# A fused two-layer block: preparing the output stage inside the stage before it, and finishing its last tile block by block

## The reference, cut to what matters

```
xn = layernorm(x)
x  = x + attention(xn) + gated_ffn(xn)                       # first layer
xn = layernorm(x)                                            # second layer; what follows is the change's place
proj = xn @ in_proj_w.T                                      # gate, conv channels, dt
y    = state_space_scan(silu(conv(proj)))                    # 128 heads, 8 groups, done over 8 chunks of 128 tokens
g    = y * silu(gate)                                        # 1024 tokens x 8192
g    = g / sqrt(mean(g*g over the group) + eps) * norm_w     # 8 groups of 1024 channels
a    = g @ out_w.T                                           # 8192 -> 512
base = xn @ W.T + bias                                       # the adapter layer's plain part
lora = (xn @ lora_A.T) @ (2 * lora_weights * lora_B)         # 128 rows between (8 adapters of rank 16)
out  = x + a + base + lora
```

## Time and profile before

| what | us |
|---|---|
| median of 3 executions | 2231.82 (2231.77 to 2232.87) |
| the profiled execution: its own time | 2228.98 |
| the profiled execution: its span | 2227.0 |
| last matmuls of the scan begin | 1829.15 |
| last small sums on PE begin, the only PE work up to the next row | 1835.64 |
| first LoRA matmul of the output stage begins | 1849.14 |
| first matmul on gated rows begins | 1858.62 |
| last matmul begins | 2218.32 |

### The profile page before, as it was taken

One profiled execution on the slowest core, in us unless ns is written; L12 is line 12 of the kernel. 1 busy time (PEld: TensorE's weight loads), 2 busy tenths in 40 slices (PEclk: granted clock), 3 DMA queues, 4 the chain that ended last, 5 costly groups with the idle time before them and its releaser, 6 DMA issues. The chain is left out here.

```text
span 2227.0 us, 37068 instructions
## 1 busy us (share of the span) xinstructions
PE 2108.4 (95%) x12040; PEld 1562.7 (70%) x12040; DVE 1462.8 (66%) x1813; ACT 1353.2 (61%) x2384; POOL 861.2 (39%) x758
## 2 busy tenths in 40 slices
PE   6879999898999999999999999999999987999998
PEld 4634444476777777777777777777777756888886
DVE  4446666284568677778778587786787764555555
ACT  2145555433588878888787787877888762233332
POOL 1011111121157666657666575665667570000000
PEclk9989999999999999999999999999999998999999
DMA  3422322223445445445454454455454557444462
GB/s 132 161 75 71 82 76 61 74 95 95 119 131 161 158 148 175 145 140 184 134 165 154 145 166 154 140 168 153 150 177 148 159 181 256 141 139 139 141 217 76
DMA packets 184055, 310.81 MB, mean 140 GB/s; under 512 B 20512, under 2 KB 96800, under 8 KB 183744
## 3 DMA queue, kind: packets, MB, share of 16 engines
q1 hardware_dynamic: 183872, 308.53, 44.7%
HBM read 252.52 MB, written 55.68 MB: 138 GB/s over the span
## 5 line engine op out<-in xcount | busy, mean ns | idle before, releaser
L145 PE MATMUL ssm_pp<-xhi,ssm_lo 128*128 128x512 f32 x1192 | 479.4, 402 | 4.7 <-DVE ssm_bc L1541 3.5
L147 PE MATMUL ssm_pp<-xhi,ssm_hi 128*128 128x512 f32 x1192 | 466.2, 391 | 0.0
L146 PE MATMUL ssm_pp<-xlo,ssm_hi 128*128 128x512 f32 x1192 | 465.6, 391 | 0.0
L1443 ACT ACTIVATE ssm_sct<-ssm_cumb,ssm_gpar 128x128 f32<-128x128 f32 x1024 | 312.9, 390 | 53.5 <-DMA ssm_cumb<-dt_sums 28.5
L1541 DVE SCALAR_TENSOR_TENSOR ssm_xc<-ssm_pp,vectors,ssm_xc 128x1022 f32<-128x1022 f32 (+2 forms) x192 | 245.1, 1277 | 47.3 <-ACT ssm_xc L1402 32.3
L137 POOL TENSOR_TENSOR ssm_lo<-ssm_raw,ssm_hi 128x512 fp32r<-128x512 f32 x149 | 238.0, 1602 | 93.1 <-ACT ssm_hi L126 93.1
L145 PEld LDWEIGHTS ssm_pp<-xhi,ssm_lo 128*128 128x128 f32 x1192 | 224.0, 188 | 69.0 <-issue 20.9
L147 PEld LDWEIGHTS ssm_pp<-xhi,ssm_hi 128*128 128x128 f32 x1192 | 224.2, 188 | 48.1
L146 PEld LDWEIGHTS ssm_pp<-xlo,ssm_hi 128*128 128x128 f32 x1192 | 224.3, 188 | 42.8
L1576 DVE TENSOR_TENSOR ssm_sct<-ssm_sct,ssm_cbm 128x1024 f32<-128x1024 f32 x128 | 224.5, 1754 | 40.5 <-ACT ssm_sct L1450 27.8
L1708 POOL TENSOR_TENSOR ssm_go<-ssm_t,ssm_gt 128x512 f32<-128x512 f32 x128 | 165.1, 1290 | 201.3 <-DVE ssm_t L1612 201.3
(11 more groups left out here) (210 smaller groups left out, 4011.8 us busy)
## 6 DMA issues: line engine op xcount, KB each, us to landing
ssm_cumb<-dt_sums SPq DMA_DIRECT2D x96, 1024.0 KB, 6.1
ssm_raw<-w SPq DMA_DIRECT2D x149, 256.0 KB, 5.6
gated<-ssm_go SPq DMA_DIRECT2D x128, 256.0 KB, 4.6
out_graw<-gated SPq DMA_DIRECT2D x64, 512.0 KB, 4.2
out_raw<-w SPq DMA_DIRECT2D x65, 256.0 KB, 2.7
ssm_cumb<-dt_sums SPq DMA_DIRECT2D x32, 512.0 KB, 4.0
ffn_raw<-w SPq DMA_DIRECT2D x37, 256.0 KB, 2.8
stk_qs<-qk_parts SPq DMA_DIRECT2D x96, 64.0 KB, 2.2
```

The costliest lines, as they stand in the source:

```text
L145: pe.matmul(out, wlo, xhi, start=start, stop=False)
L146: pe.matmul(out, whi, xlo, start=False, stop=False)
L147: return pe.matmul(out, whi, xhi, start=False, stop=stop)
L1443: i = act.activation(sct[:, s % 2, h, :], cumb[:, s % 2, 0, h, :], ACT.Relu, scale=-1.0, bias=gpar[:, unit, 0, s % NTOK, h:h + 1])
```

## The change

- The lora_A tile becomes the last of the five extra tiles, and lora_B becomes a sixth weight tile of the state-space feed (load, high part on ACT, low part on POOL, in slot 2 of its ring). PE multiplies nothing with it in that stage.
- The product with lora_A is not stored to `base`. ACT (`lora_high`, in the place of the fifth `copy_pre`) and DVE (`lora_low`, behind the last `finish`) read it from PSUM, scale it by the coefficient and write the two halves into slots 0 and 1 of the same ring. The coefficient is made early in the stage by DVE.
- The output stage's semaphores live through both stages, and POOL clears 30 of them at the start of the state-space stage. The clearing block and its barrier are gone.
- SP no longer waits at the end of the state-space stage. In the output stage it waits for `rstd` and `gated` before it loads them, for `squares` in step 0 of the first group, and for `base` in the last group.
- The work on group 7's 1/sqrt moves to later steps (sum from the start to j = 2, square root to j = 3, reciprocal from j = 2 to j = 4, its store from j = 3 to j = 5).
- In the last of the 64 tiles PE goes by output block with both batches inside, and signals each block. DVE takes a block when it is signalled.

```diff
@@ emit_ssm @@
-            return not (last and ... r[0] >= G) or r[1] < NPRE
+            return not (last and ... r[0] >= G) or r[1] <= NPRE
 ...
-            base_out(NPRE - 1)
             squares_out(G - 1, 0)
             out(G - 1, NS - 1)
             squares_out(G - 1, 1)
-            for q in g_out:
-                sp.wait_ge(q, G * NS // 2 * 16)
-            sp.wait_ge(rms_out, 16)
-            sp.wait_ge(pre_out, NPRE * 16)
-            sp.wait_ge(var_out, 2 * G * B * 16)
 ...
+            def lora_high():
+                act.wait_ge(dt_dve, 6 + NTOK)
+                act.wait_ge(tile_done, G * GT + NPRE)
+                act.activation(lora_h[0], slot(NE + NPRE - 1), ACT.Copy, scale=lc[:, 0:1]).then_inc(marks.lora_hi, 1)
 ...
+            def lora_low():
+                dve.wait_ge(marks.lora_hi, 1)
+                dve.scalar_tensor_tensor(lora_h[1], slot(NE + NPRE - 1), lc[:, 0:1], lora_h[0].bitcast(F32),
+                                         ALU.mult, ALU.subtract).then_inc(marks.lora_lo, 1)
 ...
+            for s in marks.cleared:
+                pool.sem_clear(s)
             for r in range(feed.begun, rank(FIRST, is_tile) + AHEAD):
                 low((0, r))
@@ emit_out, before its block @@
-        with nc.Block() as clear:
-            @clear.gpsimd
-            def _(pool):
-                for s in mine:
-                    pool.sem_clear(s)
@@ emit_out, SP @@
-            sp.dma_start(h[:], c.pre_dram[0]).then_inc(h_in, 16)
             load_w(0, 0)
+            sp.wait_ge(m.rms_out, 16)
             sp.dma_start(rs[:, 0, :], c.rs_dram[0].partition_broadcast(P)).then_inc(rstd_in, 16)
+            for q in m.g_out:
+                sp.wait_ge(q, NB * 16)
             load_g(0, 0)
             load_w(0, 1)
             load_g(0, 1)
-            load_w(0, 2)
-            for unit in range(2):
-                sp.dma_start(halves[:, unit, :], over_partitions(c.var_dram[unit, G - 1:G])).then_inc(sq_in, 16)
+            for q in m.g_out:
+                sp.wait_ge(q, G * NB * 16)
@@ emit_out, PE @@
+                if last:
+                    for o in range(KT):
+                        for b in range(B):
+                            mm = part(*args, o, b, False, True)
+                        mm.then_inc(sums_done, 1)
+                    return
 ...
-            pe.wait_ge(h_lo_done, 1)
-            spread(0, 0, h_hi, h_lo, True, False)
+            q = NPRE % lora.slots
+            h_hi, h_lo = (half[:, 0:2, :].rearrange("p s t -> p (s t)") for half in (lora.hi, lora.lo))
+            for b in range(B):
+                for o in range(KT):
+                    part(lora.hi[:, q, :], lora.lo[:, q, :], h_hi, h_lo, o, b, True, False)
@@ emit_out, DVE @@
-            dve.wait_ge(tile_done, PRE + G * NB)
             dve.wait_ge(base_added, KT)
             for o in range(KT):
+                dve.wait_ge(sums_done, o + 1)
                 dve.scalar_tensor_tensor(x[:, o, :], ps[:, o, :], c.vec[:, V_OB + o:V_OB + o + 1], x[:, o, :],
                                          ALU.add, ALU.add).then_inc(added, 1)
```

More of the change, by code:

```diff
@@ L1060, in exists @@
         def exists(r, last):
-            return not (last and isinstance(r[0], int) and r[0] >= G) or r[1] < NPRE
+            return not (last and isinstance(r[0], int) and r[0] >= G) or r[1] <= NPRE
         def made(e, last):
@@ L1069, in pre_dst @@
         def pre_dst(i):
-            return xc[:, 0, i, :] if i < CU else gt[:, 0, 0, :]
+            return xc[:, 0, i, :]
         def conv_col(g, e):
@@ L1818, in body @@
                     if not (first and j < 2):
-                        load_w(g, PRE + j)
+                        load_w(g, j)
                     if not (last and j + 2 >= NB):
                         load_g(g, j + 2)
+                    if first and j == 0:
+                        sp.wait_ge(m.var_out, 2 * G * B * 16)
+                        for unit in range(2):
+                            sp.dma_start(halves[:, unit, :], over_partitions(c.var_dram[unit, G - 1:G])
+                                         ).then_inc(sq_in, 16)
                     if first and j < G - 1:
@@ L1926, in body @@
                     if j == 2 and isinstance(g, int) and not last:
+                        dve.wait_ge(sq_in, 32)
+                        dve.tensor_tensor(sums[:], halves[:, 0, :], halves[:, 1, :], ALU.add).then_inc(sq_sum, 1)
+                    if j == 4 and isinstance(g, int) and not last:
                         dve.wait_ge(std, 1)
```

128 lines of the change are left out of this document (66 added, 62 removed).

## The result

| what | before | after |
|---|---|---|
| median of the executions timed side by side, us | 2231.82 (2229.59 to 2236.74, 5) | 2215.96 (2215.1 to 2221.35, 5) |
| ratio | | 0.9941, 95% interval 0.9925 to 0.9956 |
| the profiled execution: own time, span | 2228.98, 2227.0 | 2215.61, 2213.9 |
| issue of the last squares to the first load of the output stage | 4.16 | 0.73 |
| ... to the first LoRA matmul | 10.64 | 0.78 |

The account below looks back on a forecast made before the run. PE was taken to bound the kernel, gapless in the output stage's long part, so gains lie at its edges: 3.8 + 3.8 - 0.2 = 7.4 us, 2231.8 to 2224.4 us. Range: 2222.5 to 2226.5; 8 in 10: 2219.0 to 2227.8.

Parts of the forecast that it names:

- The block's entry: Start of the output stage: without the 0.8 us wait and 2.5 us clearing block, the first load comes 3.3 us earlier.
- The LoRA rows: Output stage's first 24 matmuls: start at 1839.4 instead of 1849.1, take 7.6 us from half clock, end at 1847.0.
- The first gated tile: After the LoRA rows: tile 1 lands at 1849.45, PE starts gated rows at 1852.8; gain at this edge 3.8 us.
- 512 KB at 403 GB/s are 1.3 us: Load queue at the output stage's start: dropping out_h brings the second load of gated rows 1.3 us earlier.
- The rival with faster loads: Output stage's start: loads avoid the small-load slowdown, PE starts at 1849.9; edge gives 8.7, sum 12.3 us; chance 0.18.
- Group 7's 1/sqrt: First steps of the output stage: moving this work by two steps was costed at nothing.
- The second start at half clock: First gated tile: after 5.8 us of PE idleness the clock is at half again, charged 2.0 us.
- No part of the change touches what is in that stretch: Long part of the output stage, 1536 matmuls at 0.2344 us: claimed untouched by the change, so no gain or loss.
- The last tile: End of the output stage: only the fourth block's addition and store follow the last matmul; gain 3.8 us.
- The state-space stage: Stage before the output stage: POOL's added low part delays ssm_xw and may hold PE; loss 0.2 us, bounds 0 and 1.3.
- contention rule: State-space stage: GpSimd contends with two-input DVE instructions, so the new low part holds DVE; sum up to 1.3 us smaller.
- The sum: Whole kernel: 3.8 + 3.8 - 0.2 = 7.4 us, span 2219.6 us, median 2224.4 us; the forecast had chance 0.60.

Follow-up runs that it names:

- clears_back: The changed kernel with the block clearing the output stage's semaphores, and its barrier, back between the stages; ratio to the kernel before 0.9955.
- wait_back: The changed kernel with SP's waits for all its stores back at the end of the state-space stage; ratio to the kernel before 0.9954.
- lora_reload: The changed kernel, again loading 512 KB from base first and splitting it into unused tiles, LoRA matmuls waiting for that; ratio to the kernel before 0.9961.
- halves_late: The changed kernel with the two small loads of squares, and SP's wait for them, two steps later; ratio to the kernel before 0.9957.
- kept_warm: The changed kernel with 12 more LoRA matmuls ahead of the real ones, result unchanged; ratio to the kernel before 0.9948.
- tail_only: The kernel before with only the last tile changed, to go by output block with its signals and DVE waits; ratio to the kernel before 0.9975.
- low_late: The changed kernel with POOL making the low part of lora_B behind its last squares; ratio to the kernel before 0.9944.

## Why the prediction was right in direction and wrong in size

- **The block's entry, forecast 3.3 us earlier: right.** The first load moved from +4.16 to +0.73, 3.4. clears_back puts the block at 2.2 where 2.5 was forecast, wait_back the wait at 0.8 to 0.9.
- **The LoRA rows: right.** They start at the barrier, at half clock, and end near 1846.8; 1847.0 was forecast.
- **The first gated tile: right chain, wrong landing.** "512 KB at 403 GB/s are 1.3 us" is the first step that failed: taking out_h away was worth 2.77 us of landing time (lora_reload). The rows of tile 1 landed 8.7 us behind the first load where 10.1 was forecast; with out_h back they took 11.5, as before (11.4). DVE multiplied tile 1 at 1847.86 instead of 1849.45, and PE started at 1851.03 instead of 1852.8. The rival with faster loads gave 8.7 us for this edge, for a cause that halves_late refutes; that its sum of 12.3 lies near the measured 13.2 is chance, since the spacing made up the difference.
- **Group 7's 1/sqrt, "I cost it at nothing": incomplete.** Its sum had held tile 1's multiplication by 1.2 us before. The forecast has this gain without naming it: it goes from the landing straight to the 3.3 us of the chain, where before had 1.26 us in between (1854.05 to 1855.31).
- **The second start at half clock: right in kind,** 1.38 instead of 2.0, and 1.4 to 2.8 over the profiles; kept_warm shows that it goes with the idle time. With the landing, the entry gave 6.15 instead of 3.8.
- **"No part of the change touches what is in that stretch": wrong, 2.9 us.** This is the second step that failed. The instructions are the same, but SBUF addresses are not, by 32 bytes. It is the largest error of the sum, which put the term at nothing. It is a lucky one: the same edit could have moved the rows to a worse distance.
- **The last tile: right,** 3.9 against 3.8, in tail_only too.
- **The state-space stage: the path was right, the size too small,** 1.05 us by low_late against 0.2, inside the bounds of 0 and 1.3. The pair of profiles before and after shows none of it, since the first profile of before was long in this step. By the nearest rows I had taken the delay of `ssm_xw` for covered; it was 1.27 of low part and 0.86 of a slower `ssm_sqs`. The prediction gave the contention rule of the Trainium skill, GPSIMD Engine Reference, section 1, as one by which DVE would be held. The trace agrees, and both engines pay. Over the stage of the changed kernel that DVE product takes 1.21 to 1.23 us in the 33 cases with no POOL operation beside it, and 2.31 (median) in the 57 with POOL busy throughout it; POOL's decay of the state takes 1.05 to 1.07 us in the 16 cases without that product beside it and 1.97 to 2.05 in the other 48. So the spread of the earlier trace rows goes with POOL. In the rows above, at the one place that counts, it was POOL that paid (1.32 for 0.46, 2.04 for 1.06), while DVE's product took 1.34 and 1.38 us. By the rule the prediction had a loss of up to 1.3 us more than its 0.2; low_late puts the whole loss at 1.05.
- **The sum:** entry 6.15, spacing 2.9, end 3.9, and 0.1 ahead of them in these two profiles: 13.1 us of span instead of 7.4. The median fell 15.9 us, 2.8 more. No experiment explains these 2.8; they are of the size of the spread of executions, and the interval of the ratio (9.8 to 16.7 us) covers them. So of the 8.4 us by which the median missed the forecast, 5.7 are terms of the sum, 2.9 of them the spacing and 2.35 the entry, and 2.8 are not explained.

## What to carry to other kernels

When an edit adds or removes any SBUF tile, compare the spacing of matmuls in a stretch that it doesn't touch, and try to put weights and moving operands a multiple of 256 bytes apart. Price a load at the head of a queue by what the same place of the trace needs for its bytes, not by the rate of a full stream. And when work is moved ahead of a barrier, look at the idle time that it leaves behind: here a filler of 12 matmuls cost nothing that the profile shows and kept the clock. Look also at what stands ahead of the critical operation in its engine's order: a small sum that waited for small loads held it by 1.2 us.

## What the runs showed of the hardware

- The spacing of 128x512 fp32r matmuls with a weight load each was 0.2267, 0.2324 or 0.2333, 0.2343 and 0.2333 us at 0, 128, 160 and 192 bytes (modulo 256) between weights and moving operand in SBUF, 3.4% between best and worst, 12 us in this stage. Not told apart: which of the two reads is held, and why one distance has two spacings. Distance 256 rests on one profile.
- DVE's product of two SBUF tiles (128x1024) took 1.22 us alone and 2.31 with POOL busy throughout it, POOL's decay (128x512) 1.06 without that product and 2.04 mostly with it.
- About 3 us behind the stage's first load the DMA rate dipped to 188 (after) and 147 GB/s (halves_late) for a microsecond, with the small loads near and without them; a little later it is back at 395 to 405 (after). The broadcast of `rstd` was a common load; it was not taken away, so that it is the cause is only argued.
